# Sorting the edge list by one-hot products in place of a DRAM table, in a graph layer with layer norm

## What is computed

```python
hx = jnp.einsum('ni,rio->rno', x, weight)
msg = hx[edge_type, src]
agg = jax.ops.segment_sum(msg, dst, num_segments=num_nodes)
node_repr = agg * 0.5 ** 0.5 + h_bias
node_repr = node_repr + (x @ loop_weight) * 0.5 ** 0.5
return _layernorm(x + node_repr, axis=-1)
```

## Time and profile before

| | |
|---|---|
| median of 3 runs | 781.48 us |
| lowest and highest run | 780.89 and 785.09 us |
| span of the profiled execution | 1004.9 us (no further time is recorded for it) |
| mean granted TensorE clock in it | 0.854 |
| busy: PE, DVE, ACT, POOL | 728.6, 587.2, 506.7, 537.1 us |
| DMA | 173.8 MB, 173 GB/s over the span |
| packets under 512 B | 28994 of 82706 |

### The profile page before, as it was taken

One profiled execution on the slowest core, in us unless ns is written; L12 is line 12 of the kernel. 1 busy time (PEld: TensorE's weight loads), 2 busy tenths in 40 slices (PEclk: granted clock), 3 DMA queues, 4 the chain that ended last, 5 costly groups with the idle time before them and its releaser, 6 DMA issues. The chain is left out here.

```text
span 1004.9 us, 18114 instructions
## 1 busy us (share of the span) xinstructions
PE 728.6 (73%) x4680; PEld 662.7 (66%) x4680; DVE 587.2 (58%) x1911; ACT 506.7 (50%) x1089; POOL 537.1 (53%) x610
## 2 busy tenths in 40 slices
PE   4643324899987778786877889887778777568880
PEld 4522213799977677786866779886668766567770
DVE  6621003899964355564555568876666655565771
ACT  2310102788865455454544457764646554555662
POOL 1677776100166656765666566365555556555633
PEclk9855556899998988987989899997898888898996
DMA  5511102777765555655564565765466556466531
GB/s 201 194 43 43 43 1 93 243 253 273 265 205 183 184 159 191 182 196 177 184 200 167 174 199 178 260 193 179 157 204 194 160 192 201 156 203 209 187 145 45
DMA packets 82706, 173.78 MB, mean 173 GB/s; under 512 B 28994, under 2 KB 45092, under 8 KB 82635
## 3 DMA queue, kind: packets, MB, share of 16 engines
q1 hardware_dynamic: 59675, 125.35, 37.1%
q0 software_dynamic: 22960, 47.58, 15.0%
HBM read 100.92 MB, written 78.67 MB: 179 GB/s over the span
## 5 line engine op out<-in xcount | busy, mean ns | idle before, releaser
L971 DVE TENSOR_TENSOR y_out<-y_ps,bias_b 128x512 f32<-128x512 f32 x196 | 134.3, 685 | 212.8 <-remote 153.9
L1193 PE MATMUL y_ps<-w_low,xt_high 128*128 128x256 f32 x768 | 253.0, 329 | 5.3 <-issue 5.1
L1104 ACT ACTIVATE y_out<-y_out,shift,rstd 128x256 f32<-128x256 f32 x392 | 216.7, 590 | 52.5 <-issue 37.1
L1193 PE MATMUL y_ps<-w_high,xt_high 128*128 128x256 f32 x768 | 230.8, 300 | 10.1 <-issue 10.1
L1193 PE MATMUL y_ps<-w_high,xt_low 128*128 128x256 f32 x768 | 231.1, 301 | 3.6 <-issue 3.2
L1170 PE MATMUL xt_ps<-ident,x_in 128*128 128x128 f32 x784 | 135.1, 301 | 121.5 <-DVE xt_low L892 54.2
L892 DVE TENSOR_TENSOR xt_low<-xt_ps,xt_high 128x512 fp32r<-128x512 f32 x221 | 150.2, 679 | 107.3 <-ACT xt_high L1053 73.2
L1053 ACT ACTIVATE xt_high<-xt_ps 128x512 fp32r<-128x512 f32 x221 | 129.1, 585 | 142.5 <-remote 108.8
L1170 PEld LDWEIGHTS xt_ps<-ident,x_in 128*128 128x128 f32 x784 | 102.7, 155 | 145.2 <-issue 89.7
L624 POOL DMA_INDIRECT gathered<-in_x,src_stage x106 | 109.2, 1030 | 130.5 <-PE xt_ps L1170 95.0
L1193 PEld LDWEIGHTS y_ps<-w_low,xt_high 128*128 128x128 f32 x768 | 161.3, 210 | 8.5 <-issue 7.8
(11 more groups left out here) (122 smaller groups left out, 927.7 us busy)
## 6 DMA issues: line engine op xcount, KB each, us to landing
x_in<-in_x SPq DMA_DIRECT2D x97, 512.0 KB
out_rows<-y_out SPq DMA_DIRECT2D x97, 512.0 KB
message_in<-message_rows SPq DMA_DIRECT2D x100, 128.0 KB
keys<-padded_dst SPq DMA_DIRECT2D x13, 508.0 KB
w_rel<-in_L_gnn_weight SPq DMA_DIRECT2D x1, 2048.0 KB, 14.3
gathered<-in_x,src_stage POOLq DMA_INDIRECT x106
message_rows<-message_out,edge_stage POOLq DMA_INDIRECT x106
grouped<-entry_stage,place_stage POOLq DMA_INDIRECT x98
```

The lines of the kernel that those rows point to most:

```text
L971: nc.vector.tensor_tensor(to, y_ps[q][:, :].rearrange("p (t d) -> p t d", t=2), bias_2, ALU.add).then_inc(moved, 1)
L1104: a = nc.scalar.activation(y_tile(p, t), y_tile(p, t), ACT.Identity, scale=rstd[:, slot, i:i + 1], bias=shift[:, slot, i:i + 1])
L1193: return nc.tensor.matmul(to, xt[:, q, t * D + k * P:t * D + (k + 1) * P], w, start=start, stop=stop)
```

## The change

The DRAM table goes. Where an edge of column c has tile `hi` and lane `lo`, the sorted list of sources is the sum over the columns of the product of two 128-row matrices: one has a 1 in column `lo` of the edge's row, the other the edge's source in column `hi`. The edge numbers are formed likewise, beside the sources, so each column is one fp32 product of 128x128 with 128x212, and all 98 add up in one PSUM tile (`sorted_ps`). POOL builds the lane matrices (128x128) and the edge-number half of the tile matrices (128x106), DVE the source half (128x106), seven columns at a time in two buffers that lie in the still unused `w_rel_high` and `w_rel_low`. That makes 14 groups. In the phase of 19 main pairs behind the first 8, at pair k, PE multiplies group k-1 behind its own pair's product, and DVE builds group k. DVE then copies both lists out of PSUM; an entry without an edge gets the mark SKIP. The first message pair may come after 27 main pairs.

The order of pairs becomes: 8 main; 19 main; 26 times "gmm" (message pairs plain); 27 times "gmm" (all split); 13 main ("pause"); fix stage as before. The first 8 pairs are no hardware loop any more.

```diff
-MORE = 2
+GROUP = 7
-    pause = MAIN - 8 * first - MORE - 8 * turns - 2 * mix_rest - FPAIRS
+    GROUPS = EC // GROUP
+    sort_pairs = GROUPS + 5
+    mix_first = MPAIRS // 2
+    pause = MAIN - FIRST - sort_pairs - 2 * MPAIRS - FPAIRS
-    mix, mix_at = "gmgmgmm" * turns, 2
+    sort_at, mix_at = 1, 2
+    mix = "gmm" * mix_first
...
-    for kinds, n, plain in (("m" * 8, first, PLAIN),
-                            ("m" * MORE, 1, ()),
+    for kinds, n, plain in (("m" * FIRST, 1, PLAIN),
+                            ("m" * sort_pairs, 1, range(0, sort_pairs, 2)),
                             (mix, 1, places(mix, "g")),
-                            (mix, 1, ()),
-                            ("gmm" * mix_rest, 1, ()),
+                            ("gmm" * (MPAIRS - mix_first), 1, ()),
...
+        lane_of = w_rel_high[:, 0:2 * GROUP * P].bitcast(F32).rearrange("p (c l) -> p c l", l=P)
+        tile_of = w_rel_low[:, 0:2 * GROUP * 2 * MTP].bitcast(F32).rearrange("p (c v m) -> p c v m", v=2, m=MTP)
+        sorted_ps = misc_ps[:, 0:2 * MTP]
+        def columns(k):
+            return [(k * GROUP + i, (k % 2) * GROUP + i) for i in range(GROUP)]
...  POOL
-            pool.wait_ge(table_blank, 16)
-            def write_columns(i):
...
-            write_columns(0)
-            with pool.Fori(1, EC // (2 * SORT_PER)) as i:
-                write_columns(i)
-            for half in range(2):
-                pool.wait_ge(columns_written[half], 16 * EC // 2)
-            nc.gpsimd.dma_start(list_at.rearrange("p k n -> p (k n)"), grouped.rearrange("(p k) n -> p (k n)", p=P)).then_inc(list_loaded, 16)
-            pool.wait_ge(list_loaded, 16)
+            for k in range(GROUPS):
+                if k >= 2:
+                    pool.wait_ge(group_sorted, k - 1)
+                for c, slot in columns(k):
+                    last = nc.gpsimd.tensor_scalar(lane_of[:, slot, :], iota_f[:, :], lo_f[:, c:c + 1], None, ALU.is_equal)
+                last.then_inc(lanes_built, 1)
+                for c, slot in columns(k):
+                    last = nc.gpsimd.tensor_scalar(tile_of[:, slot, 1, :], iota_f[:, 0:MTP], hi_f[:, c:c + 1], e1_f[:, c:c + 1],
+                                                   ALU.is_equal, ALU.mult)
+                last.then_inc(edges_built, 1)
+            pool.wait_ge(list_ready, 2)
...  DVE, called in each step behind low() and prepare()
+            def sort(k):
+                if k is None:
+                    return
+                if k < GROUPS:
+                    if k >= 2:
+                        dve.wait_ge(group_sorted, k - 1)
+                    for c, slot in columns(k):
+                        last = nc.vector.tensor_scalar(tile_of[:, slot, 0, :], iota_f[:, 0:MTP], hi_f[:, c:c + 1], src_f[:, c:c + 1],
+                                                       ALU.is_equal, ALU.mult)
+                    last.then_inc(sources_built, 1)
+                if k == GROUPS + 1:
+                    dve.wait_ge(group_sorted, GROUPS)
+                    nc.vector.tensor_copy(src_at[:, :], sorted_ps[:, 0:MTP]).then_inc(list_ready, 1)
+                    link(nc.vector.tensor_scalar(empty[:, :], sorted_ps[:, MTP:2 * MTP], 0.0, float(SKIP), ALU.is_equal, ALU.mult))
+                    nc.vector.tensor_tensor(edge_at[:, :], sorted_ps[:, MTP:2 * MTP], empty[:, :], ALU.add).then_inc(list_ready, 1)
...  ACT, ahead of the first write into w_rel_high
+                    act.wait_ge(group_sorted, GROUPS)
...  PE, behind multiply() in each step
+                k = sort_step(p)
+                if k is not None and 1 <= k <= GROUPS:
+                    pe.wait_ge(lanes_built, k)
+                    pe.wait_ge(edges_built, k)
+                    pe.wait_ge(sources_built, k)
+                    for c, slot in columns(k - 1):
+                        last = nc.tensor.matmul(sorted_ps, lane_of[:, slot, :], tile_of[:, slot, :, :].rearrange("p v m -> p (v m)"),
+                                                start=c == 0, stop=c == EC - 1)
+                    last.then_inc(group_sorted, 1)
```

More of the change, by code:

```diff
@@ L324, in gnn_layernorm_kernel @@
         rel_i, src_i, pos_i, hi_i, lo_i, e1_i = (scratch(EC, I32) for _ in range(6))
-        rel_f, pos_f, hi_f, lo_f, e1_f, dead, place_f = (scratch(EC) for _ in range(7))
-        place_i = scratch(EC, I32)
+        rel_f, pos_f, hi_f, lo_f, e1_f, dead, src_f = (scratch(EC) for _ in range(7))
         onehot, running, placed = (scratch(R * EC) for _ in range(3))
@@ L337, in gnn_layernorm_kernel @@
         key_f, next_f, key_eq, key_at = (scratch(P) for _ in range(4))
-        blank = scratch(2 * MTP, I32)
+        empty = scratch(MTP)
         loop_raw = scratch(KT * D)
@@ L356, in gnn_layernorm_kernel @@
         places_ready = sem("places_ready")
[L357 to L360, removed]
+        lanes_built = sem("lanes_built")
+        edges_built = sem("edges_built")
+        sources_built = sem("sources_built")
+        group_sorted = sem("group_sorted")
+        list_ready = sem("list_ready")
         keys_ready = sem("keys_ready")
@@ L441, in has_carry, with prepare_step @@
             return t == 0 or nth(p, "f", 1) is not None
+        def prepare_step(p):
+            return p.j if p.at == 0 else None
         def sort_step(p):
-            return p.j if p.at == 0 and not p.looped and p.s == 0 else None
+            return p.j if p.at == sort_at else None
+        lane_of = w_rel_high[:, 0:2 * GROUP * P].bitcast(F32).rearrange("p (c l) -> p c l", l=P)
[3 more added lines that the diff above has]
+            return [(k * GROUP + i, (k % 2) * GROUP + i) for i in range(GROUP)]
         def list_step(p):
@@ L630, in _ @@
             pool.wait_ge(places_ready, 1)
-            pool.wait_ge(table_blank, 16)
-            def write_columns(i):
-                for half in range(2):
[L635 to L645, removed]
-                    for k in range(half * SORT_PER, (half + 1) * SORT_PER):
-                        nc.gpsimd.indirect_dma_start(grouped, bass.IndirectOffsetOnAxis(ap=place_stage[:, k:k + 1], axis=0),
-                                                     entry_stage[:, k, :], None,
-                                                     bounds_check=P * MTP - 1, oob_is_err=False).then_inc(columns_written[half], 16)
@@ L844, in prepare @@
                     link(nc.vector.tensor_copy(lo_f[:, :], lo_i[:, :]))
-                    link(nc.vector.scalar_tensor_tensor(out=place_f[:, :], in0=lo_f[:, :], scalar=float(MTP), in1=hi_f[:, :], op0=ALU.mult, op1=ALU.add))
-                    nc.vector.tensor_tensor(place_i[:, :], place_f[:, :], dead[:, :], ALU.add).then_inc(places_ready, 1)
+                    nc.vector.tensor_tensor(hi_f[:, :], hi_f[:, :], dead[:, :], ALU.add).then_inc(places_ready, 1)
+                    dve.wait_ge(places_ready, 1)
                 if k == 3:
@@ L946, in step @@
                 low(p.ahead(2))
-                prepare(sort_step(p))
+                prepare(prepare_step(p))
+                sort(sort_step(p))
                 prepare_lists(list_step(p))
```

35 lines of the change are left out of this document (11 added, 24 removed).

## The result

The changed kernel takes 849.9 us (median of 4; 847.8 to 852.6), the kernel before 781.4 us: a ratio of 1.087, 95% interval 1.083 to 1.090. The forecast was 754 us with a range of 732 to 790. The change makes the kernel 68 us slower.

A forecast was written before the change was run, and what follows sets the result against it. POOL's serial steps were taken to bound the kernel (777 of 781.5 us). First message product at 117, triples 318, pause 27, fix stage and tail 287 made 749, 28 less than 777, so 754 us, range 732 to 790.

The forecast's parts named there:

- The profiled execution is not the timed one: Whole kernel before: profiled span 1004.9 us, timed median 781.5, so 223 us of the profile are not in the timed runs.
- the ledger: Whole kernel before: least time POOL's steps allow, 777 us, 4.5 under the median; sort and gathers to 180, message stage to 478.
- The crawl: Sort phase, 57 to 165 us: main pairs slow beside the small scatters, PE busy 32 of 108 us; gain counted without it.
- The rival that the crawl was in the timed runs: Sort phase: the crawl also slows timed runs and goes with the change, giving 725 to 740 us; chance 0.12.
- PE's products: Sort phase: seven fp32 products per group at 0.36 us each, 2.5 us; bounds 3.0 and 5.0 us.
- POOL's builds: Sort phase: fourteen operations per group at 0.25 us, 3.5 us; bounds 0.15 and 0.5 us per operation.
- POOL builds slowly: Sort phase rival: 0.5 us per operation, 7.0 us per group, 790 us; decides from 0.31 us per operation; chance 0.08.
- The port between DVE and POOL: Sort phase: DVE's seven builds could each delay POOL by 0.21 us, 5.0 us per group, 8 us more; left to the range.
- What the tie costs: Sort phase: PE's waits ahead of each group's products hold back everything behind; no term, with PE setting the 4.4 us step.
- The triples: Message stage: 53 sets of one message and two main pairs at 6.0 us, 318 us; bounds 5.65 and 6.33.
- dense stage too slow: Message stage rival: 2.35 us per pair set by ACT, DVE and DMA together, 374 us for 318, total 810; chance 0.12.
- Pause, fix stage, tail: After the message stage: 13 pause pairs at 2.1 us, 27 us; fix stage and tail as before, 287 us.

The follow-up runs named there:

- the second profile of the kernel before: The kernel before, unchanged, profiled again: 780.7 us, span 778.4; pause 20 us where the ledger had 12, fix stage and tail 279 where it had 287.
- lanes_on_dve: The changed kernel with the lane matrices built by DVE in seven small comparisons per group, POOL building only the edge halves: 809.0 us, ratio 1.032.
- The order and the products alone: Two runs against the kernel before: only the new pair order, sort still by scatters, 856.9 us; only the sort products, old pair order, 852.1 us.
- Repairing the two failed terms: Changed kernel, message pairs plain, lane matrices by one broadcast DVE comparison per group: 771.8 us; also without the unread split of the relation weights: 768.2 us.

## Why the prediction was wrong

Step by step, in the order of the forecast:

- **"The profiled execution is not the timed one", and the ledger.** Right, and confirmed by the second profile of the kernel before: 479 and 778 us for 478 and 777, with the two errors named there. (Its side sum for the profiled execution took 2.84 us per pair where 322 us for 112 pairs are 2.88, and 4.4 us for a step where 1.97 + 2.5 is 4.5. Neither matters.)
- **The crawl.** Right in leaving it out of the timed runs, and wrong in calling it "a crawl beside the small scatters": in the second profile the same scatters run beside main pairs at full pace. The rival that the crawl was in the timed runs is refuted.
- **PE's products.** Right: 0.36 us forecast for one, 2.7 us for seven found at full clock (2.5 forecast), 4.2 to 5.3 in seven of the 14 groups, behind waits of 2.8 to 4.7 us, at a mean granted clock of 0.50 to 0.65.
- **DVE's builds.** 1.83 us for seven, 1.5 forecast: 0.26 each from start to start. Nearly right, and from the third group on never the last to be ready.
- **POOL's builds.** The step that failed. I took 0.25 us for an operation, from an affine select of the same shape, and wrote 0.5 us as the bound from above. The runs show 0.597 and 0.742 us, 9.2 us per group for 3.5. An affine select and a comparison of the same shape cost 0.29 and 0.60 us, so a shared shape said nothing about the cost. The rival "POOL builds slowly" was the right one, its limit of 0.31 us too. But its price was worked out at 0.5 us (790 us), and its chance set at 0.08, on no more than one row; at 9.2 us per group the same sum gives 754 + 14 x 4.8 = 821 us. POOL's 14 groups end at 156.5 us where the forecast had the sort finished at 105, and the first message product comes at 174.6 and not at 117.
- **The port between DVE and POOL.** By the rule in the prediction DVE's seven builds would have held up POOL by 1.5 us per group. The group shown above has POOL at 5.12 us beside them, against 4.97 (7 x 0.71) for builds beside nothing: 0.15 us. With twice as many builds on DVE (`lanes_on_dve`) it is about 0.5 us per group, still far from the builds' own length.
- **What the tie costs.** I named PE's wait ("everything" stands behind it) and gave it no term in the sum, because PE was to be the slowest. That condition was the POOL price again. The order and the products alone show what is at stake: 39 main pairs, 78 us by 2.0 us each, in which the old sort was hidden free of charge.
- **The triples.** The second step that failed. 6.0 us forecast. Plain triples: 6.27 beside the split of the relation weights, 6.0 without it, so the size was right. Split triples: 7.28, above my bound of 6.33. I had added up each engine's work and not followed a pair through DVE and ACT. And the bound was read from the last five triples of the kernel before, where 66 main pairs stand ahead and the two main pairs of a triple are normalised together; the change made that number odd. The first 26 triples cost about 7 us over the forecast, the last 27 about 33. The rival "dense stage too slow" was partly right: its sign was met (triples over 7 us, POOL idle for 42% of the time), and ACT and DVE, which it named, set the pace. But it is no rate per pair, it is one ring, and one plain pair in three loosens it; no run shows the DMA in it.
- **Pause, fix stage, tail.** +12 for the pause (15 forecast), +2 for the rest (0 forecast).

In the table of stages the forecast has -63, +20, +15 and 0 (117 for 180, 318 for 298, 27 for 12), together -28; the runs have -5.5, +59.9, +12.3 and +1.9. So the step that failed first, POOL's builds, is worth 57.5 us, the triples 39.9, the other two -2.7 and +1.9: together 96.6 us, and the medians are 96 over the forecast. Repairing the two failed terms gave 771.8 and 768.2 us, 14 to 18 us above the forecast of 754 for the change as written. The repaired idea brought 10 and 14 us, between a third and half of the promised 28.

## What to carry to other kernels

An operation that no trace shows on its engine deserves a wide bound from above: at 14 operations per step, 0.45 us for the 0.25 assumed was by the prediction's own sum enough to turn the gain into a loss. Ask of a slow serial step what runs beside it before removing it: the sort's 137 us on POOL cost almost nothing as long as 66 independent pairs covered it, and a faster method that puts an in-order engine behind it can cost more. In a dense stage, follow one tile round all engines in their program order: a ring of two engines that wait for each other sets a period that no busy share shows. Before an operation is moved to relieve an engine, look which engine's work is ready last.

## What the runs showed of the hardware that I had not expected

- From one start to the next, POOL takes 0.49 us for a comparison of 128x128 with an immediate, 0.58 with a column, 0.54 and 0.71 for 128x106 with two operations and two immediates or two columns. Its affine select of 128x128 lasts 0.29 us, and the same comparison with a column on DVE takes 0.21 from start to start.
- The comparison that lasts 0.60 us on POOL lasts 1.32 and 2.08 us beside DVE's two-input operations on 784 columns, and 0.60 beside DVE's one-input reduction of as many.
- One broadcast comparison of 128x896 on DVE takes 1.10 us, where seven of 128x128 take 1.6 us in all. It takes 0.5 us off DVE and adds about 0.7 us to the build of POOL beside it.
- Two profiled executions of one kernel had spans of 1004.9 and 778.4 us, with the same work of POOL in the same places and the other engines crawling in the first. What caused the first is open: no run here repeated it. A span far above the timed median is a reason to take no rate from that profile.
